# A batch-pipelined attention and expert block: k's spread transfers ahead of q's low stack, and all four on SyncE in the opening

## The reference

```python
h = _layernorm(x) * (1 + ca) + sa
q, k, v = [(h @ W.T + b).reshape(B, T, 16, 8).transpose(0, 2, 1, 3) for W, b in (Q, K, V)]
q, k = _apply_rope(q, cos, sin), _apply_rope(k, cos, sin)
scores = jnp.einsum('bhqd,bhkd->bhqk', q, k) / sqrt(8)          # causal mask, then softmax
x = x + ga * ((softmax(scores) @ v) @ Wo.T + bo)
h = _layernorm(x) * (1 + cb) + sb
x = x + gb * top2_of_8_experts(h)                               # 128 -> 512 -> 128, gelu
```

## Time and profile before

| | us |
|---|---|
| median of 3 executions | 536.73 (536.02 to 537.96) |
| the profiled execution, own time | 538.26 |
| its span | 536.5 |
| TensorE (PE) busy | 459.6 |
| VectorE (DVE) busy | 397.1 |
| ScalarE (ACT) busy | 314.8 |
| GpSimd (POOL) busy | 327.9 |

### The profile page before, as it was taken

One profiled execution on the slowest core, in us unless ns is written; L12 is line 12 of the kernel. 1 busy time (PEld: TensorE's weight loads), 2 busy tenths in 40 slices (PEclk: granted clock), 3 DMA queues, 4 the chain that ended last, 5 costly groups with the idle time before them and its releaser, 6 DMA issues.

```text
span 536.5 us, 12559 instructions
## 1 busy us (share of the span) xinstructions
PE 459.6 (86%) x3543; PEld 336.3 (63%) x3543; DVE 397.1 (74%) x1198; ACT 314.8 (59%) x853; POOL 327.9 (61%) x465
## 2 busy tenths in 40 slices
PE   4478999899989989989989988789977879999980
PEld 3245565555655655655655654479876768999970
DVE  3678898799999999999999898834425633444684
ACT  4465666565555555555555555566656546887860
POOL 3144464556966966966966957834855673445781
PEclk9999999999999999999999999979999897999995
DMA  4335644545745745745746853422222232222744
GB/s 117 99 105 155 146 139 130 136 127 163 195 125 170 194 131 164 194 129 166 195 130 157 169 152 71 125 67 57 70 62 59 86 85 56 67 66 69 246 148 140
DMA packets 77987, 67.89 MB, mean 127 GB/s; under 512 B 10915, under 2 KB 71591, under 8 KB 77920
## 3 DMA queue, kind: packets, MB, share of 16 engines
q1 hardware_dynamic: 71696, 56.91, 40.7%
q0 software_dynamic: 4320, 8.47, 4.8%
q10 hardware_dynamic: 1904, 1.70, 1.0%
HBM read 25.47 MB, written 12.05 MB: 70 GB/s over the span
## 4 chain that ended last, share of the span: by engine, by line
PE 38%; DVE 31%; issue 14%; POOL 4%; ACT 4%; DMA 3%; another core or an unknown queue 3%; SPq 1%; DVEq 1%; ACTq 1%; POOLq 0%
DVE maxima L1429 8%; PE ps_sc L1608 8%; PE misc L1760 5%; PE misc L1598 4%; PE ps_pv L1714 4%; PE ps_max L1598 4%; PE ps_sc L1685 3%; DVE shifts L1443 2%; PE ps_max L1667 2%; ACT after_k L859 2%; DVE turned_a L1380 2%; DVE z L1039 2%; DVE stats L1024 2%; DVE low L1387 2%
## 5 line engine op out<-in xcount | busy, mean ns | idle before, releaser
L933 ACT ACTIVATE probs<-ps_sc 128x512 f32<-128x512 f32 x192 | 108.1, 595 | 61.6 <-PE ps_sc L1685 52.0
L1429 DVE TENSOR_REDUCE maxima<-ps_max 128x2 f32<-128x512 f32 (+1 forms) x192 | 130.2, 682 | 16.7 <-PE ps_max L1669 9.8
L751 POOL DMA_INDIRECT results<-after_k,after_e x71 | 70.0, 986 | 66.6 <-DVE after_k L1124 46.8
L1685 PE MATMUL ps_sc<-q_diags,k_stacks 128*128 128x512 f32 x192 | 97.4, 508 | 5.6 <-ACT probs L933 3.6
L761 POOL TENSOR_SCALAR_AFFINE_SELECT probs<-probs 128x512 f32<-128x512 f32 x128 | 81.6, 644 | 27.3 <-ACT probs L933 26.1
L1608 PE MATMUL ps_sc<-wproj_s,after_k 128*128 x568 | 81.0, 287 | 1.3 <-ACT after_k L859 0.7
L1608 PEld LDWEIGHTS ps_sc<-wproj_s,after_k 128*128 128x128 f32 x568 | 71.7, 198 | 5.9 <-issue 3.3
L711 POOL DMA_INDIRECT sorted_rows<-rows,slots x64 | 65.9, 1030 | 14.6 <-issue 10.0
L1124 DVE SCALAR_TENSOR_TENSOR after_k<-ps_sc,after_e,after_k 128x128 f32<-128x128 f32 x71 | 24.8, 349 | 64.3 <-PE ps_sc L1608 34.5
L1667 PE MATMUL ps_max<-k_diags,q_stacks 128*128 128x512 f32 x128 | 61.1, 478 | 2.1 <-DVE maxima L1429 1.9
L1117 DVE COPY after_k<-wfc_s 128x644 f32 x71 | 37.3, 528 | 25.9 <-issue 25.6
(11 more groups left out here) (180 smaller groups left out, 912.6 us busy)
## 6 DMA issues: line engine op xcount, KB each, us to landing
q_diags<-q_stacks SPq DMA_DIRECT2D x64, 128.0 KB
k_diags<-k_stacks SPq DMA_DIRECT2D x62, 128.0 KB
gate_now<-gate_rows SPq DMA_DIRECT2D x16, 320.0 KB
after_e<-sorted_rows SPq DMA_DIRECT2D x71, 65.0 KB
k_stacks<-high SPq DMA_DIRECT2D x32, 128.0 KB
q_stacks<-high SPq DMA_DIRECT2D x30, 128.0 KB
x_in<-in_x SPq DMA_DIRECT2D x16, 128.0 KB, 3.3
k_stacks<-low SPq DMA_DIRECT2D x16, 128.0 KB
```

The source lines that it names most:

```text
L751: nc.gpsimd.indirect_dma_start(result_dram, bass.IndirectOffsetOnAxis(ap=row_in[m % RING][:, D + 1:D + 2].bitcast(U32), axis=0), y_out[m % ...
L933: nc.scalar.activation(probs[:, g % 2, c], ps_sc[u % 2][:], ACT.Exp, scale=SCALE).then_inc(S["exp_done"], 1)
L1429: nc.vector.tensor_reduce(to, of, AX, ALU.max).then_inc(S["max_done"], 1)
L1685: last = nc.tensor.matmul(ps_sc[u % 2][:].rearrange("p (w q) -> p w q", w=4), k_stack[(s.t + d) % 3][:, g, keys * P:(keys + 1) * P], q_dia ...
```

## The change

In the steps, `spread_k` is called ahead of `stack_q_low`. In the opening, SyncE issues all four of k's spreads and ScalarE none. No instruction is added or dropped in sum.

```diff
-                        for w in range(2 if s.t == -1 else 4):
+                        for w in range(4):
                             at = slice(ROWS * w, ROWS * (w + 1))
                             sp.dma_start(k_diag[(s.t + 1) % 2][at, :, w, :].bitcast(F32), k_stack[(s.t + 1) % 3][at].bitcast(F32)
                                          ).then_inc(S["k_spread"], 16)
...
                 stack_k()
                 stack_q_high()
+                spread_k()
                 stack_q_low()
-                spread_k()
                 spread_q()
...
-                act_e.wait_ge(S["k_stacked"], 48)
-                act_e.wait_ge(S["ones_in"], 16)
-                act_e.wait_ge(S["cleared"], 4)
-                for w in (2, 3):
-                    at = slice(ROWS * w, ROWS * (w + 1))
-                    act_e.dma_start(k_diag[0][at, :, w, :].bitcast(F32), k_stack[0][at].bitcast(F32)).then_inc(S["k_spread"], 16)
```

## The result

The change is faster: 535.20 us (median of 20 runs) against 537.26 us for the kernel before beside it, a ratio of 0.9952 with a 95% interval of 0.9928 to 0.9975, or −2.6 us. The ratio is that of the means; the two medians differ by 2.1. The forecast was 533.8 us, with a range of 531.9 to 536.5. In two later sets, each on a chip of its own, the ratio came out at 0.9928 [0.9894, 0.9961] and 0.9921 [0.9904, 0.9938]. The profiled execution took 535.86 us, its span 534.1.

What follows compares the result with a forecast made beforehand. Nothing idles long (TensorE 86% busy, VectorE 74%), so only three waits for k's spread, 6.4 us, could pay. Terms −1.4 −0.2 −1.3 = −2.9 us, from the median 536.73 to 533.8 us, range 531.9 to 536.5.

Steps and rivals of the forecast that it cites:

- Term 1: Opening: without two spread issues ScalarE clears sooner, so the first matmul and k's projection start sooner; −1.4 us, between −1.2 and −1.41.
- Term 2: End of step 0: k's spread lands sooner, but q's low stack and VectorE's maximum then bind; −0.2 of the 0.78 us wait.
- second rival: The shift is taken back by TensorE's slow clock, or waits only change their name; about 536.2 us, chance 0.17.
- Term 3: End of step 3: k's spread, even with its long issue, lands before TensorE is free; −1.3 us, between 0 and −1.32.
- The first rival: Only the opening pays: step 3's long issue is an accident or moves where it hurts; −1.6 us, 535.1, chance 0.25.
- The other steps: Steps besides 0 and 3: q's low stack and q's spread come later but are covered; nothing gained, nothing lost, price 0.
- The slower rival: q's low stack, behind four 128 KB transfers, becomes the bound; +3.5 us net, 540.2, chance 0.07.
- point of decision: Landing time of q's low stack, from about 4.1 us, at which its becoming the bound decides the outcome.
- its price, +6.2: With landings of 4.5 us, steps 0 and 1 lose 1.5 each and some eight steps like step 7 lose 0.4 each.
- The signs I named: Changed kernel's expected times: clearing 22.95, first matmul 25.3 to 25.5, projection 26.9, step 1 at 43.3, step 4 at 97.9.
- the signs of being wrong: L1660 late for q's low stack, step 4 starting at 99.2 or later, or the shift gone by 340 us.

Runs made afterwards that it cites:

- the table's three profiles: Profiles of the kernel before and of the change, one each on three chips; the change's ratios there were 0.9952, 0.9928 and 0.9921.
- the halves: The change with the opening's k spreads cut into two 64 KB halves, the second awaited only by step 0's seventh product; 513.98 us, ratio 0.9936 to the kernel before.
- the extra transfer: The change plus one 128 KB transfer from k's stack to memory, ahead of k's four spreads in the opening; 512.64 us (one run).
- one pairing of profiles: New order in the steps alone, opening as before (513.15 us, ratio 0.9900), laid beside the change's profiles with the same 1.10 us for four matmuls.
- the kernel of the two steps: The change with the new order in steps 0 and 3 alone, the other steps in the old order; 515.08 us, ratio 0.9940 to the kernel before.
- opening alone: The kernel before with SyncE issuing all four of the opening's k spreads, steps in the old order; 517.42 us, ratio 1.0007.
- the first pair: The first profiles of the kernel before and of the change, from the first set; ratio 0.9952, 535.20 us against 537.26.
- step 3 put back: The change with the old order (q's low stack ahead of k's spread) in step 3 alone; 536.88 us, ratio 0.9960 to the kernel before.
- the change's third profile: The change unaltered, run again on the third set's chip; ratio 0.9921 to the kernel before.

## Why the prediction was right, and where it was not

The direction and the size were right: −2.9 forecast, −2.6 measured, and −3.9 and −4.1 by the ratios of the other two sets. That the sum came out is in part luck: its errors cancelled. The means of the table's three profiles each, and the time from first issue to first matmul, split the 3.7 us that the change gains by step 15: opening −0.2, step 0 −1.1, step 1 −1.0, step 2 −0.25, step 3 −1.1, steps 4 to 14 −0.1. Step 1's share is no removed wait, but a slow stretch of TensorE that the profiles of before have and those of the change do not; see below.

- **Term 1, the opening: −1.4 forecast; −0.2 for the matmul, some −0.35 for the projection behind it (it is part of step 0's −1.1), nothing shown in the time.** The failed step is "The last one of before started at about 23.64 and the matmul at 26.61, 2.97 later; so the matmul can start at 25.3". That took the landing to follow the last issue at a fixed distance. Seven transfers of 128 KB were issued within 3.5 us, though, and the DMA engines were nearly full in both kernels (the change, then before):

```profile
22.00:24.00 2.00, 0.00 (x0) 0.00 (x0) 1.22 (x7) 2.00 (x3) 0.00 (x0) 0.50 0.96 246
```
```profile
22.00:24.00 2.00, 0.27 (x2) 0.00 (x0) 1.36 (x7) 0.00 (x0) 0.00 (x0) 1.00 0.94 219
```

  That the bytes awaited set the landing, the halves say (0.92 us sooner); the extra transfer did not bear it out for q's low stack, so it is likely, not shown. What is shown is that an earlier last issue hardly brought the landing forward: issued at 22.12 instead of 23.70 it took 3.95 us to land, and the matmul came 0.4 sooner. ScalarE's chain did move: the fill of `v_wide` was 2.6 us sooner, in the means of three profiles 1.9. But the projection of k starts 1.01 us after the matmul in all three profiles of the change, and in those of before 1.65, 1.01 and 1.38: ScalarE's two issues had cost TensorE 0.6, 0 and 0.4 us. I took the first for the rule. By the page DMA: Bandwidth & Descriptors of the Trainium skill, section Issuing engines are not separate DMA queues, the term was near nothing; the time of this part alone agrees (1.0007), though in part because TensorE waited for the landing anyway, and in one pairing of profiles 0.9 us were there.
- **Term 2, the end of step 0: −0.2 forecast; about −1.1 in step 0.** The arithmetic of the new order was right: the wait left is 0.6 to 0.85 us, for VectorE's maximum or q's low stack. (Its two things come at one time: in the profile of the change q's low stack had landed by 42.47, VectorE's maximum was done at 42.49, and the matmul starts at 42.55.) What was wrong is the 0.78 as the size of the old wait. TensorE's slow stretch from 39 us in that one execution hid the rest; with a clean end of step 0 the wait is 1.83 or 1.84 (three profiles). The note in the second rival, 0.4 more if the stretch does not come, went the right way and was too small.
- **The slow stretch itself (second rival, 0.17).** Where it falls into steps 0 and 1 it costs 0.8 to 1.6 us, by the lengths of those steps with and without it; step 1's −1.0 is this alone. One such stretch beyond 36 us stands in all three profiles of before (39 to 42.4, 44.2 to 47.7, 45 to 48.4), and in none of the nine profiles that have the new order in steps 0 to 2; but the kernel of the two steps, with the opening and the end of step 0 of the change, has one from 37.6 to 41, and the one with the opening alone, which waits 1.84 us, has none. In the first profile of before it came ahead of the long wait, so the wait cannot have brought it on there. Whether the change removes it, and with it about 1 us of the gain, stays open. The Trainium skill, TensorE: Matmul & The Clock Gate, section Part 1: The HAM clock gate, has the moment of the clock's change vary from run to run; the runs agree: in three executions of the changed kernel the four matmuls at 31.5 to 31.8 us took 1.10, 1.10 and 2.04.
- **Term 3, the end of step 3: −1.3 forecast; −1.1 in the mean, −1.5 in the first pair.** Right. The delay is not an accident, only its size varies: in the five profiles with the old order in step 3 the wait was 1.32, 0.69 and 0.86 (before), 1.42 (opening alone) and 1.47 us (step 3 put back). The mechanism was not quite the one forecast, though: the sum kept the long issue and gave it room, but in the new order no long issue stands in k's spread of step 3, so whether the room would have covered one was never tried. The first rival (only the opening pays) is refuted the hard way: the opening is the part that pays least.
- **The other steps: 0 forecast.** Held for steps 4 to 14 (219.9 us in both, in the mean); step 2 gains 0.25, which I had not seen.
- **The slower rival.** Its point of decision is a landing of 4.1 us. In the first profile that was passed in the opening alone (4.5), where k's spread was the later one; in the steps it took 2.1 to 2.6 in eleven of fifteen, and 3.9 at most. But in the change's third profile it took 4.5 us at the end of step 11, and the rival came true once:

```profile
254.28 0.65 SPq L544 DMA_DIRECT2D q_stacks<-low  x1
...
258.84 1.23 SPq L573 DMA_DIRECT2D q_diags<-q_stacks  x2
...
258.91 0.47 PE L1654 MATMUL ps_max<-k_diags,q_stacks 128*128 128x512 f32 x1 [0.81 <-DVE maxima L1423]
```

  That step lasts 19.84 us instead of 18.78, the next one 19.97 instead of 21.5, so nothing is lost. (The wait is put down to VectorE, whose maximum was done at 258.26; q's low stack landed at 258.82.) And its price, +6.2, was wrong by much where it was tried, in steps 5 to 13: with q's low stack 2.5 us later the matmul lost 6.4 us in five places and the kernel 0.7 by step 15. For steps 0 and 1, 3.0 of the 6.2, it was not tried.

The signs I named: ScalarE's clearing at 22.95 (21.73) and the projection at 26.9 (27.22), step 1 at 43.3 (42.55), step 4 at 97.9 (96.71), the tiles 2.9 sooner (3.5), no wait for k's spread after the opening (true), the matmul at 25.3 to 25.5 (26.21, wrong). Of the signs of being wrong one came: in two of the change's three profiles L1654 waits for q's low stack at the end of step 0, by 0.67 and 0.85 us. It did little harm: VectorE's maximum was done only 0.04 and 0.2 us ahead of that landing.

## What to carry to other kernels

A wait read from one profile is a lower bound when a slow stretch of the waiting engine lies just ahead of it: ask how long the wait would be if that engine had been on time. Before a transfer is credited with the time of its issues, look at the share of the DMA engines in that stretch; here, at 0.94 to 0.96, issuing the last one 1.6 us sooner moved the matmul by 0.4, and awaiting half of the bytes moved it by 0.9. In the later steps here a stall at the end of the short step of a pair was mostly made good in the next one, so the price of a wait is found by what the later steps do, not by its length; the wait of step 3 was not made good (step 4 lasts 19.8 us with it and without). And two profiles are compared only when TensorE's clock rose at the same time in both: the opening's part showed 0.9 us or nothing, by the pairing.

## What the runs showed of the hardware

SyncE's issue of a 128 KB transfer takes 0.60 us in the median, and eight to thirteen of SyncE's 300 to 350 issues in the attention phase, of all sizes, take 1.0 to 2.1 us. About half of these long ones stand 10 to 25 transfers apart, the others 4 to 113, and they are often where they stand in other executions too; in a changed order others are hit. What causes them was not tried. With seven transfers of 128 KB issued within 3.5 us, two of them landed 3.95 and 4.5 us after issue; the last of four in the steps took 2.50 and 2.57, and q's low stack there 2.1 to 2.6 in eleven of fifteen. And a granted clock of 1.00 beside four 128x256 matmuls at 2.04 us instead of 1.10 was seen in several executions: the durations are the surer reading.
